# Neighbour maximum of a four-layer graph network on one core: one fused operation per chunk and head in place of subtract, share and maximum

## The reference

```python
s_i = jnp.einsum('hnd,hd->nh', logx, att[:, :DH])
s_j = jnp.einsum('hnd,hd->nh', logx, att[:, DH:])
alpha = jax.nn.leaky_relu(s_i[dst] + s_j[src], 0.2)
m = jax.ops.segment_max(alpha, dst, num_segments=n)
a = jnp.exp(alpha - m[dst])
ssum = jax.ops.segment_sum(a, dst, num_segments=n)
a = a / jnp.clip(ssum[dst], MIN_NORM)
```

## Time and profile before

| | |
|---|---|
| median of 3 runs | 9486.06 us (9477.93 to 9505.69) |
| the profiled execution | 9485.6 us |
| its span, first to last instruction | 9483.6 us |
| mean granted TensorE clock | 0.690 |
| VectorE busy | 3947.4 us (42%), 8209 instructions |
| ScalarE busy | 1803.0 us (19%), 6789 instructions |
| GpSimd busy | 5163.3 us (54%), 5240 instructions |
| moved by DMA | 997.00 MB, mean 105 GB/s |

### The profile page before, as it was taken

The page is one execution under the profiler, slowest core; times in us unless marked ns, Lnnn a source line. Parts: engine busy times, 40 slices in busy tenths (PEclk is TensorE's granted clock), DMA queues, the critical chain, the costliest instruction groups (busy, mean ns, idle before and its releaser), DMA issues. The chain is left out here.

```text
span 9483.6 us, 78659 instructions
## 1 busy us (share of the span) xinstructions
PE 4045.1 (43%) x14501; PEld 2859.4 (30%) x14502; DVE 3947.4 (42%) x8209; ACT 1803.0 (19%) x6789; POOL 5163.3 (54%) x5240
## 2 busy tenths in 40 slices
PE   4000035555476676875454410000046663845444
PEld 2000024444355555433333300000034552333332
DVE  5000023333355555432222367777776666222223
ACT  0000001111100000220000014444446663100000
POOL 5777756666666666126666407777721110166665
PEclk7555567677788888986666655555578887967666
DMA  3000012222255555233333315555553333333334
GB/s 101 3 14 6 3 61 87 88 87 88 102 173 172 171 174 172 48 140 91 92 91 90 71 49 179 180 179 177 178 124 113 115 113 92 134 89 92 91 90 86
DMA packets 390541, 997.00 MB, mean 105 GB/s; under 512 B 133180, under 2 KB 167648, under 8 KB 383836
## 3 DMA queue, kind: packets, MB, share of 16 engines
q0 software_dynamic: 227264, 559.12, 21.0%
q1 hardware_dynamic: 163228, 437.33, 14.0%
HBM read 684.30 MB, written 311.78 MB: 105 GB/s over the span
## 5 line engine op out<-in xcount | busy, mean ns | idle before, releaser
L797 POOL DMA_INDIRECT rel_rows<-relation_rows,rel_ring_row x1664 | 1612.8, 969 | 1400.0 <-ACT rel_ring_end L781 903.2
L809 PE MATMUL rel_sums<-rel_rows,rel_hot 128*128 128x256 f32 x3328 | 1199.9, 505 | 1235.8 <-issue 705.5
L809 PEld LDWEIGHTS rel_sums<-rel_rows,rel_hot 128*128 128x128 f32 x3328 | 817.1, 253 | 1619.5 <-issue 1428.7
L1635 POOL DMA_INDIRECT nmax_rows<-messages,nmax_ring_row x832 | 878.2, 1056 | 653.6 <-ACT nmax_ring_row L1582 393.4
L621 POOL DMA_INDIRECT rows_by_src<-spread_rows,spread_ring_place x832 | 814.0, 978 | 488.3 <-issue 244.6
L694 POOL DMA_INDIRECT both_rows<-batch_normed,both_ring_row x832 | 816.6, 982 | 458.6 <-issue 232.7
L488 POOL DMA_INDIRECT records_by_dst<-sort_ring_rec,sort_ring_place x784 | 836.5, 1067 | 293.1 <-issue 234.5
L599 PE MATMUL spread_p_r<-g_big,spread_hot_t 128*128 x1664 | 632.0, 546 | 561.5 <-ACT spread_hot_t L543 397.7
L833 DVE TENSOR_TENSOR g_acc<-rel_sums,g_acc 128x256 f32 x832 | 351.2, 422 | 1209.1 <-remote 581.8
L706 PE MATMUL both_out_sums<-both_out_rows,both_out_hot 128*128 128x257 f32 x1664 | 515.8, 465 | 405.0 <-DVEq L743 378.4
L1818 PE MATMUL att_sums<-att_weighted,att_hot 128*128 128x260 f32 x1664 | 542.3, 482 | 312.4 <-DVE att_weighted L1888 169.9
(11 more groups left out here) (384 smaller groups left out, 6784.1 us busy)
## 6 DMA issues: line engine op xcount, KB each, us to landing
both_out_rows<-rows_by_src SPq DMA_DIRECT2D x208, 520.0 KB
kept_rows<-nmax_rows SPq DMA_DIRECT2D x208, 520.0 KB
att_rows<-kept_rows SPq DMA_DIRECT2D x208, 520.0 KB
rel_rows<-relation_rows,rel_ring_row POOLq DMA_INDIRECT x1664
relation_rows<-mix_table SPq DMA_DIRECT2D x25, 1024.0 KB
relation_rows<-rel_table SPq DMA_DIRECT2D x25, 1024.0 KB
rows_by_src<-spread_rows,spread_ring_place POOLq DMA_INDIRECT x832
both_rows<-batch_normed,both_ring_row POOLq DMA_INDIRECT x832
```

The costliest lines, as they stand in the source:

```text
L797: pool.indirect_dma_start(rows[:, j, 0:words], None, table, bass.IndirectOffsetOnAxis(ap=ring_row[:, j:j + 1], axis=0)).then_inc(landed[r] ...
L809: last = nc.tensor.matmul(sums[:, 2 * r + q // 2, 0:width], hot[:, j, :], rows[:, j, :], start=q % 2 == 0, stop=q % 2 == 1)
L1635: pool.indirect_dma_start(rows[:, j, :], None, msg_dram.ap(), bass.IndirectOffsetOnAxis(ap=ring_row[:, j:j + 1], axis=0)).then_inc(landed[ ...
```

## The change

The sign is turned: the running result `low` is the smaller of itself and distance minus score, starts at +2^100 in place of -2^100, and is negated at the end. VectorE does both steps in one SCALAR_TENSOR_TENSOR per chunk and head, 128x128, whose scalar is the score, one per partition: 16 per group, 64 per turn, 3328 in all. `PER` becomes 16. ScalarE's `share`, the buffers `short` and `shared` and the semaphore `shares` go, and ScalarE's program is the refills alone, with the first four ahead of the loop. Before each operation VectorE waits until all but its last three are done, so that the same region's former operation, four back, has ended. GpSimd's and SyncE's programs are as before.

```diff
--- before.py
+++ after.py
@@ -1545,26 +1545,24 @@
-    PER = GRP * 2 - 1
+    PER = GRP * H
     with ExitStack() as ctx:
         m = Mem(nc, ctx, "nmax")
         rows = m.sb("rows", [P, BODY, D + H])
         ring_row = m.sb("ring_row", [P, BODY], I32)
         away = m.sb("away", [P, BODY, P])
-        short = m.sb("short", [P, 2, H, P])
-        shared = m.sb("shared", [P, 2, H, P])
         minus_local = m.sb("minus_local", [P, CHP])
         best = m.sb("best", [P, T, H])
         tmp = m.sb("tmp", [P, T, H])
         rest = m.sb("rest", [P, (T + 1) * 2 * H])
         p_t = m.ps("p_t", [P, 2, H, P])
-        staged, tick, taken, vec, shares, turn, reduced, placed, away_ready = (m.sem(n) for n in (
-            "staged", "tick", "taken", "vec", "shares", "turn", "reduced", "placed", "away_ready"))
+        staged, tick, taken, vec, turn, reduced, placed, away_ready = (m.sem(n) for n in (
+            "staged", "tick", "taken", "vec", "turn", "reduced", "placed", "away_ready"))
         landed = [m.sem(f"landed_{r}") for r in range(RING)]
         stored = [m.sem(f"stored_{r}") for r in range(RING)]
         kept_at = kept_dram.ap().rearrange("(p c) w -> p c w", c=CH)
         block = ctx.enter_context(nc.Block())
-        high = g.big[:, 0:(T + 1) * H * P].rearrange("p (t h n) -> p t h n", h=H, n=P)
+        low = g.big[:, 0:(T + 1) * H * P].rearrange("p (t h n) -> p t h n", h=H, n=P)
         @block.sync
         def _(sp):
@@ -1591,39 +1589,18 @@
                                                 bias=minus_local[:, bass.ds(at + q, 1)])
                 last.then_inc(away_ready, 1)
-            def share(i, r):
-                act.wait_ge(landed[r], i * (16 * GRP) + 16 * GRP)
-                act.wait_ge(away_ready, i * RING + (r + 1))
-                if not (isinstance(i, int) and i * RING + r < 2):
-                    act.wait_ge(taken, i * (RING * PER) + (r - 1) * PER)
-                q = r * GRP + GRP - 1
-                for h in range(H):
-                    last = nc.scalar.activation(shared[:, r % 2, h, :], away[:, q, :], ACT.Identity, scale=-1.0,
-                                                bias=rows[:, q, D + h:D + h + 1])
-                last.then_inc(shares, 1)
-
             def refill(i, r):
                 act.wait_ge(taken, i * (RING * PER) + (r + 1 - RING) * PER)
                 act.wait_ge(stored[r], i * 16)
                 stage(i * BODY + r * GRP, r)
                 distance(i * BODY + r * GRP, r)
-            def turn_of(i, first=False, last_turn=False):
-                share(i, 0)
-                if not first:
-                    refill(i, RING - 1)
-                for r in range(1, RING):
-                    share(i, r)
-                    if not last_turn:
-                        refill(i + 1, r - 1)
-
             for r in range(RING):
                 stage(r * GRP, r)
                 distance(r * GRP, r)
-            turn_of(0, first=True)
-            with act.Fori(1, LOOPS - 1) as i:
-                turn_of(i)
-            turn_of(LOOPS - 1, last_turn=True)
+            with act.Fori(1, LOOPS) as i:
+                for r in range(RING):
+                    refill(i, r)
         @block.gpsimd
         def _(pool):
@@ -1640,7 +1617,7 @@
             for t in range(T):
                 pe.wait_ge(reduced, t + 1)
                 for h in range(H):
-                    last = nc.tensor.transpose(p_t[:, t % 2, h, :], high[:, t, h, :], g.ident[:])
+                    last = nc.tensor.transpose(p_t[:, t % 2, h, :], low[:, t, h, :], g.ident[:])
                 last.then_inc(turn, 1)
         @block.vector
@@ -1648,13 +1625,8 @@
             c = Count(dve, vec)
             v = Vector(nc, dve, c)
             nc.vector.tensor_scalar(minus_local[:], g.rec[0][:, :, 2], -STEP, None, ALU.mult).then_inc(placed, 1)
-            v.did(nc.vector.memset(g.big[:, 0:(T + 1) * H * P], -STEP))
+            v.did(nc.vector.memset(g.big[:, 0:(T + 1) * H * P], STEP))
             t = Count(dve, taken)
-
-            def shorten(r, q):
-                t.step(nc.vector.tensor_tensor(
-                    short[:, q % 2, :, :], rows[:, r * GRP + q, D:D + H].unsqueeze(2).broadcast_to([P, H, P]),
-                    away[:, r * GRP + q, :].unsqueeze(1).broadcast_to([P, H, P]), ALU.subtract))
             def turn_of(i):
                 t.enter(i, RING * PER)
@@ -1662,20 +1634,14 @@
                 for r in range(RING):
                     dve.wait_ge(away_ready, i * RING + (r + 1))
                     dve.wait_ge(landed[r], i * (16 * GRP) + 16 * GRP)
-                    if not (isinstance(i, int) and i + r == 0):
-                        t.wait()
-                    shorten(r, 0)
                     for q in range(GRP):
-                        if q < GRP - 2:
-                            if q:
-                                t.wait()
-                            shorten(r, q + 1)
-                        t.wait(1 if q < GRP - 2 else 0)
-                        if q == GRP - 1:
-                            dve.wait_ge(shares, i * RING + (r + 1))
-                        at = high[:, bass.ds(tiles[2 * r + q // 2], 1), :, :].rearrange("p t h n -> p (t h) n")
-                        t.step(nc.vector.tensor_tensor(
-                            at, short[:, q % 2, :, :] if q < GRP - 1 else shared[:, r % 2, :, :], at, ALU.max))
+                        for h in range(H):
+                            if not (isinstance(i, int) and i + r + q == 0):
+                                t.wait(H - 1)
+                            at = low[:, bass.ds(tiles[2 * r + q // 2], 1), h, :].rearrange("p t n -> p (t n)")
+                            t.step(nc.vector.scalar_tensor_tensor(
+                                at, away[:, r * GRP + q, :], rows[:, r * GRP + q, D + h:D + h + 1], at,
+                                ALU.subtract, ALU.min))
             turn_of(0)
             with dve.Fori(1, LOOPS) as i:
@@ -1685,12 +1651,12 @@
             dve.sem_inc(reduced, 2)
             for t in range(T):
                 dve.wait_ge(turn, t + 1)
-                nc.vector.tensor_reduce(best[:, t, :], p_t[:, t % 2, :, :], AX.X, ALU.max).then_inc(reduced, 1)
+                nc.vector.tensor_reduce(best[:, t, :], p_t[:, t % 2, :, :], AX.X, ALU.min).then_inc(reduced, 1)
             dve.wait_ge(reduced, T + 2)
             si, top = g.sm[:, 0:T, 0:H], g.sm[:, 0:T, H:2 * H]
             v.did(nc.vector.memset(g.sm[:], 0.0))
             v.did(nc.vector.tensor_copy(si, g.si[:]))
-            v.tt(best[:], best[:], g.sj[:], ALU.max)
+            v.stt(best[:], best[:], -1.0, g.sj[:], ALU.mult, ALU.max)
             v.tt(best[:], best[:], g.si[:], ALU.add)
             v.ts(tmp[:], best[:], 0.2, ALU.mult)
             v.tt(top, best[:], tmp[:], ALU.max)
```

## The result

The changed kernel takes 9698.94 us (median of 4 runs, 9693.87 to 9704.44), the kernel before, in the same set of runs, 9488.84 (4 runs, 9477.93 to 9505.69). The ratio is 1.0216, 95% interval 1.0201 to 1.0232: slower by 210 us, where 9434 us and a range of 9330 to 9620 were forecast. Its profiled execution has a span of 9696.2 us, of which the stage (gathers from 5682.1, last operation about 7146.8) is 1465 us, against 1258. Of the 213 us between the two spans 207 lie in the stage.

What follows compares the result with a forecast made beforehand. VectorE was taken to bound the stage neighbour_max by little: two turns of 33.8 + 12 = 45.8 us against 47.8, 26 x (45.8 - 47.8) = -52 us, so 9485.6 - 52 = 9434 us. The range was 9330 to 9620.

Steps and rivals of the forecast that it cites:

- A group of 16 in 4.1 us: In neighbour_max, VectorE's new operations would start about 0.25 us apart in undisturbed stretches, 16 of them taking 4.1 us.
- the sum: VectorE's undisturbed turn in neighbour_max: 64 x 0.254 + 0.62 = 16.9 us, in place of 19.9.
- Register steps hidden outside an episode: VectorE's register steps, 102 a turn after 35, were taken as hidden except in episodes, stretches where they take 0.7 us each.
- GpSimd needs 43.4: GpSimd's gathers in neighbour_max at 1.36 us a chunk would need 43.4 us for two turns, less than VectorE's 45.8.
- rival 1: GpSimd becomes the bound of neighbour_max: 114 us less, 9371 us, or 9283 with gathers at 1.25 us a chunk; chance 0.27.
- Episode loss of 12 us per two turns: VectorE's loss in neighbour_max to an episode of slow register steps, about once in two turns: 12 us in place of 8.0.
- the bound of 16: Upper bound on VectorE's loss per episode in us, all of the episode lost; the lower bound was 8.0.
- rival 2: Episodes in neighbour_max grow with register steps: loss up to 23 us per two turns, 239 us more, 9725 us; chance 0.19.
- ScalarE's share counted as nothing: Taking 16 x 0.29 us a turn off ScalarE in neighbour_max was given no gain, since VectorE sets the pace.
- Rival 3: VectorE's small operations in neighbour_max don't overlap: two turns take 56 us, 213 us more, 9699 us; chance 0.06.
- Any change outside the stage of over 20 us would speak against the account: Test of the forecast: the rest of the kernel, outside neighbour_max, should not move by over 20 us.

Runs made afterwards that it cites:

- after: The changed kernel itself, profiled for the result; median 9698.94 us, ratio 1.0216 to the kernel before.
- a0: The changed kernel run again, unaltered, at the upper level; 9663.12 us, ratio 1.0258 to the kernel before.
- p2: The changed kernel with the distances in PSUM instead of SBUF, at the upper level; 9581.48 us, ratio 1.0170 to the kernel before.
- e2: The changed kernel with the distances in PSUM instead of SBUF, at the lower level; 8516.25 us, ratio 0.9902 to the kernel before.
- g1: The changed kernel with a full wait ahead of each chunk's first operation, at the upper level; 9540.07 us, ratio 1.0128 to the kernel before.
- e4: The kernel before without ScalarE's share, VectorE doing all four subtractions of a group, at the lower level; 8617.38 us, ratio 1.0021.
- g2: The changed kernel with a full wait ahead of every second chunk, at the upper level; 9546.20 us, ratio 1.0129 to the kernel before.
- f1: The changed kernel with one full wait per chunk, none ahead of its other three operations; upper level 9440.58 us (ratio 1.0016), lower 8518.49 us (0.9904).
- h1: f1 with ScalarE's share put back for each group's fourth chunk; lower level 8540.82 and 8536.58 us, upper 9527.79 us (ratio 1.0112).
- b0: The kernel before, unaltered, profiled at the upper level; 9414.62 us (one run).

## Why the prediction was wrong

- *"A group of 16 in 4.1 us", 0.254 us apart.* Nearly right: 4.29 us, 0.262 apart, and a length of 0.346 us for the 0.334 expected. The discounted reading of the Trainium skill ("Vector Engine (DVE) Microarchitecture Reference", Points that are easy to get wrong), half the throughput with two non-bf16 sources, is not what these rows show either: from 128 to 256 columns (L1993) the length grows from 0.346 to 0.467 us, 0.95 ns a column, where half the throughput was 533 ns for 256 columns in the prediction's working, 2.08 a column. VectorE's work of a turn is 4 x 4.29 = 17.2 us for the 16.9 of the sum.
- *Register steps hidden outside an episode.* Right: 102 a turn, and the 16 operations run without a gap.
- *"GpSimd needs 43.4" (two turns at 1.36 us a gather).* **This is the step that failed first.** The duration of a gather was taken from the earlier trace rows as a property of the gather, while it depends on what VectorE runs beside it. It measured 1422 ns + 0.30 = 1.722 us a gather, 55.1 us for two turns (32 gathers), 26 x (55.1 - 47.8) = 190 us more than before, against the 207 us by which the stage grew. The earlier trace rows had the sign of it: gathers of 1.26 us beside others of 0.95, and the longer one waits for a maximum, as the line from the kernel before above shows. I read these as room to get faster (rival 1's far end, 9283) and not as a cost that a denser VectorE might raise.
- *Episode loss of 12 us per two turns.* Wrong for this kernel: `after` has 28 slow steps on VectorE in the stage and `a0` one. With VectorE idle 2.9 us in every group, they are hardly there. That the idle time keeps them away is not shown. But without the hold they come, and **here a second step failed**. `p2` needs 1385 us, 53.3 per two turns, where VectorE's work was put at 33.8: a loss of 19.5 us, above the bound of 16, and in the range of rival 2 (from 14.0). It is 12.8 us more than `e2` needs at the lower level, but that is counted from the gathers' 40.5 us and not from VectorE's work, so it does not confirm the 12. Without the hold the kernel would thus still have missed the forecast of 52 us less: `p2` is 159 us above the kernel before of its set, `g1` 117.
- *ScalarE's share counted as nothing.* Near enough at the lower level: `e4`, in which VectorE also takes over the share's subtraction, is 16 us above the kernel before.
- *Rival 3, 9699 us.* The number is the measured one by accident. Its mechanism, operations that don't overlap, is refuted by the 0.262 us spacing; they do overlap, and in such runs gathers are held. *Rival 1* named the right engine as the bound, with the opposite sign. *Rival 2* has the time of `p2`, `g1` and `g2` (159, 117 and 128 us more than the kernel before, for its 41 to 239), not of the changed kernel. Its rule, that the loss grows with the number of register steps, does not hold across `f1`, `h1` and `b0`.
- *"Any change outside the stage of over 20 us would speak against the account."* There was none: 207 of the 213 us between the two spans lie in the stage.
- *The chances.* Slower had 0.30, none of it for this mechanism. The range ended at 9620, 79 us below the result.

The arithmetic of the change itself was sound: with the distances in PSUM, or with one wait per chunk, the same operations make the kernel faster at the lower level, by 85 and 84 us. At the upper level the best of these, `f1`, is 1.0016 times the kernel before (interval 1.0006 to 1.0026), so it beats the kernel before in one condition and not in the other; against the changed kernel it wins in both (8518 for 8929, 9441 for about 9663).

## What to carry to other kernels

Where GpSimd issues gathers, the duration of one is not a constant: before an edit that makes VectorE denser, look how it spreads, set the end of each long gather against the ends of VectorE's operations, and price the spread as something that can grow. A long run of short, overlapping operations with two inputs in SBUF is the case to avoid; one input in PSUM, or a real gap every four operations, removed the hold here, and at the lower level no cost of it could be seen. And if a kernel has two levels of time, test a remedy at both: the distances in PSUM, level with the best at the lower one (ratio 0.9902), made the kernel 1.7% slower than the kernel before at the upper.

## What was unexpected of the hardware

- Every one of 4842 lengthened gathers ends 0.81 to 0.84 us after the end of a VectorE operation with two inputs in SBUF, most often the one beside which it started.
- A gather of 0.95 us can last up to 10.7 us beside VectorE, to the end of a run, and in the changed kernel 40 ns in the moment at which it starts decide it (eight operations or more into a run: 600 of 605 inside, 2 of 54 outside).
- The same kernel on chips of one kind at 8602 or 9420 us. Register steps of 0.7 us are there at the upper level alone. With the hold, the changed kernel has nearly the same stage at both, 1453 and 1460 us, as the held gathers bound it; without it the stage is 1052 or 1385 us.
- Fewer instructions and more slack on VectorE (`h1` against `f1`) made the upper level worse by 87 us and the lower by 18 to 22. The two differ in the share on ScalarE as well. What starts an episode was not found.
